# Attention of an adaLN block: batch loops written out on every engine, row sums inverted ahead of the tile copies

## The reference

```python
h = _layernorm(x, axis=-1) * (1 + ca) + sa
# attention on h
scores = jnp.einsum('bhqd,bhkd->bhqk', q, k) * scale + bias
attn = jax.nn.softmax(scores, axis=-1)
a = jnp.einsum('bhqk,bhkd->bhqd', attn, v)
...
x = x + ga * (a @ o_w.T)
h = _layernorm(x, axis=-1) * (1 + cb) + sb
x = x + gb * ffn(h)        # router, top 8 of 160 experts, shared expert
```

## Time and profile before

| | |
|---|---|
| median of 3 runs | 1016.47 us (1014.36 to 1022.89) |
| profiled execution | 1013.81 us, of which the span of the trace is 1012.0 |
| granted TensorE clock in it | 0.985 of 2.4 GHz |
| attention in the trace | from about 29 to 518 us; the experts from about 568 us to the end |
| DVE, ACT, POOL busy | 769.4, 679.4, 398.1 us |

### The profile page before, as it was taken

How to read it: one execution, slowest core, us unless ns; L and a number is a source line. 1 busy time by engine, 2 the same in 40 slices (tenths; PEclk the granted TensorE clock), 3 DMA queues, 4 the chain that set the end, 5 groups by cost and what they waited for, 6 DMA issues and landing times.

```text
span 1012.0 us, 16804 instructions
## 1 busy us (share of the span) xinstructions
PE 953.2 (94%) x4592; PEld 690.6 (68%) x4592; DVE 769.4 (76%) x1452; ACT 679.4 (67%) x1168; POOL 398.1 (39%) x260
## 2 busy tenths in 40 slices
PE   4889999899998999999969699999999999999997
PEld 2546666566665666666524578888888888888886
DVE  5757667566665666766647589999999999999997
ACT  3556666466665666666626477877777777777775
POOL 0578888688886888888910000000000000000000
PEclk9999999899999999999979899999999999999999
DMA  7885445256444445534200899999999999999991
GB/s 205 258 234 119 97 119 126 63 124 142 113 96 101 96 118 125 125 90 99 66 19 27 204 221 219 223 222 222 223 222 222 221 224 221 223 220 225 220 206 41
DMA packets 71096, 160.39 MB, mean 158 GB/s; under 512 B 10273, under 2 KB 36193, under 8 KB 60945
## 3 DMA queue, kind: packets, MB, share of 16 engines
q1 hardware_dynamic: 71056, 159.97, 70.1%
HBM read 105.60 MB, written 2.42 MB: 107 GB/s over the span
## 4 chain that ended last, share of the span: by engine, by line
PE 84%; DMA 4%; DVE 4%; issue 3%; ACT 2%; SPq 1%; POOL 1%; POOLq 0%; DVEq 0%; ACTq 0%
PE ps L620 40%; PE ps L433 11%; PE ps L420 10%; PE ps L409 5%; PE ps L411 5%; PE ps L383 4%; PE ps L446 3%; PE ps L394 2%; DMA strips<-in_L_ffn_w_down 2%; DMA k_low<-qk 1%; POOL prob L859 1%; DMA comb_rows<-strips 1%; PE ps L538 1%; PE ps L540 0%; DVE qk L959 0%
## 5 line engine op out<-in xcount | busy, mean ns | idle before, releaser
L859 POOL TENSOR_SCALAR prob<-prob,rinv 128x512 f32<-128x512 f32 x256 | 397.9, 1567 | 111.3 <-DVE rinv L993 109.1
L706 ACT ACTIVATE prob<-prob,nmax 128x512 f32<-128x512 f32 x256 | 182.9, 716 | 150.9 <-DVE nmax L976 150.8
L620 PE MATMUL ps<-hT,wT 128*128 128x512 f32 x960 | 244.2, 390 | 0.3 <-DVE wT L1145 0.3
L1164 DVE TENSOR_TENSOR PT<-v_sb,strips 128x1024 f32<-128x1024 f32 x160 | 196.0, 1225 | 41.4 <-ACT v_sb L830 28.3
L830 ACT ACTIVATE v_sb<-ps 128x1024 f32<-128x1024 f32 x160 | 164.5, 1028 | 77.9 <-PE ps L620 77.4
L620 PEld LDWEIGHTS ps<-hT,wT 128*128 128x128 f32 x960 | 180.8, 189 | 39.0 <-ACT strips L805 1.1
L620 PE MATMUL ps<-stack,wT 128*128 128x512 f32 x640 | 198.1, 391 | 9.2 <-DVE wT L1151 9.2
L204 DVE COPY PT<-ps 128x512 f32<-128x512 f32 x128 | 88.4, 691 | 141.2 <-PE ps L420 138.7
L1151 DVE TENSOR_TENSOR wT<-PT,stack 128x1024 fp32r<-128x1024 f32 x160 | 195.0, 1219 | 0.0
L976 DVE CUSTOM_DVE_ANT_0 prob<-ps,strips 128x512 f32<-128x512 f32 x256 | 165.0, 681 | 11.5 <-issue 8.0
L822 ACT CAST stack<-PT 128x1024 fp32r<-128x1024 f32 x160 | 166.6, 1041 | 8.8 <-DVE PT L1164 8.8
(11 more groups left out here) (105 smaller groups left out, 731.1 us busy)
## 6 DMA issues: line engine op xcount, KB each, us to landing
strips<-comb_rows SPq DMA_DIRECT2D x158, 512.0 KB, 10.9
stack<-qk SPq DMA_DIRECT2D x128, 256.0 KB, 3.8
k_low<-qk SPq DMA_DIRECT2D x64, 128.0 KB, 3.9
hT<-qk SPq DMA_DIRECT2D x64, 128.0 KB, 3.8
strips<-bias_rows SPq DMA_DIRECT2D x3, 1792.0 KB, 13.9
strips<-in_L_ffn_w_gate SPq DMA_DIRECT2D x80, 64.0 KB, 9.8
strips<-in_L_ffn_w_down SPq DMA_DIRECT2D x80, 64.0 KB, 11.0
strips<-bias_rows SPq DMA_DIRECT2D x2, 896.0 KB, 5.4
```

Source lines behind the costliest of these rows:

```text
L620: last = nc.tensor.matmul(ps[:, bank + c, :], weights(a), rows(m, c), start=start and k == 0, stop=stop and k == 2, skip_group_check=True)
L706: nc.scalar.activation(prob[:, u, :], prob[:, u, :], ACT.Exp, bias=nmax[:, u:u + 1], scale=-1.0, accum_out=rsum[:, u:u + 1]).then_inc(s_ex ...
L859: nc.gpsimd.tensor_scalar(prob[:, u, :], prob[:, u, :], rinv[:, u:u + 1], None, ALU.mult).then_inc(s_prob, 1)
L1164: nc.vector.tensor_tensor(weighted[:, k % 4, :], silu[:, k % 2, :], cb[:, r, half * HALF:(half + 1) * HALF], ALU.mult).then_inc(s_mul, 1)
```

## The change

Three things are edited. (1) The loops over b on the five engines become Python loops: the same instructions, written out three times (GpSimd: four times), with constants in place of registers. (2) On VectorE, in each slot the inversion of two row sums stands ahead of the copies of transposed tiles (and, in slot 0, of `copy_o`); before it stood behind them. (3) `update_x` and `new_statistics` of batch b move from the end of pair 9 into pair 2 of the next batch, behind its first two `add_bias`.

```diff
-            with dve.Fori(0, B - 1) as b:
+            for b in range(B - 1):
                 for n in range(2, HPAIRS + 2):
                     pair(b, n)
...
@@ VectorE, pair(b, n)
+                if n == 2 and b >= 1:
+                    update_x(b - 1)
+                    new_statistics(b - 1)
+                invert_sums(b, n, 0)
                 if n >= 2:
                     copy_o(b, n - 2)
                 if n >= 1:
                     copy_probs(b, n - 1, 5)
-                invert_sums(b, n, 0)
...
+                invert_sums(b, n, 2)
                 if n >= 1:
                     copy_probs(b, n - 1, 7)
-                invert_sums(b, n, 2)
...
+                invert_sums(b, n, 4)
                 copy_probs(b, n, 1)
-                invert_sums(b, n, 4)
...
+                invert_sums(b, n, 6)
                 copy_probs(b, n, 3)
-                invert_sums(b, n, 6)
                 if not (final and n >= HPAIRS - 2):
                     qk_low(b, n + 2)
-                if n == HPAIRS + 1:
-                    update_x(b)
-                    new_statistics(b)
```

More of the change, by code:

```diff
@@ L291, in _ @@
             sp.dma_start(ebias[0:E - P, 1:2], expert_bias[P:E, :]).then_inc(ld["small"], 16)
-            with sp.Fori(0, B - 1) as b:
+            for b in range(B - 1):
                 for n in range(2, HPAIRS + 2):
@@ L508, in _ @@
             pe.wait_ge(ld["ow"], 16)
-            with pe.Fori(0, B - 1) as b:
+            for b in range(B - 1):
                 for n in range(2, HPAIRS + 2):
@@ L760, in _ @@
             pair(0, 1)
-            with act.Fori(0, B - 1) as b:
+            for b in range(B - 1):
                 for n in range(2, HPAIRS + 2):
@@ L857, in normalise @@
                     pool.wait_ge(s_rinv, b * (G // 2) + (UNITS * n + u) // 2 + 1)
-                    pool.sem_inc(apart, 1)
                 nc.gpsimd.tensor_scalar(prob[:, u, :], prob[:, u, :], rinv[:, u:u + 1], None,
                                         ALU.mult).then_inc(s_prob, 1)
-            with pool.Fori(0, B) as b:
+            for b in range(B):
                 for n in range(HPAIRS):
```

## The result

The changed kernel takes 1018.48 us in the median of 20 runs, the kernel before 1014.56 in 20: a ratio of 1.0044, 95% interval 1.0023 to 1.0066. It is a little slower. In the profiled executions the span goes from 1012.0 to 1016.2 us. Afterwards nine variants were measured, two of them twice. The shortest are the change without its inversion in slot 0 (0.9844 and 0.9853 of the time before) and the change with no early inversion at all (0.9843 and 0.9873); their times are not told apart. For each variant the time is a median of 4 to 8 executions, the ratio is to the kernel before as measured beside it, and the span and all rows are those of one profiled execution. The ratios leave out the few executions that fell in the chip's slower state.

The account below looks back on a forecast made before the run. TensorE was taken to bound steady pairs of 14.20 us. Terms -15.5 + 2.4 + 16.8 + 0.5 = +4.2 us gave 1018.0 from the profiled execution, 1020.7 from the median; forecast 1019, range 1001 to 1030.

Parts of the forecast that it names:

- The ring: Slot 0's early reciprocal waits for the exponential, delaying `attend` each pair: 14.8 us instead of 14.20, +16.8 us over 28 pairs.
- Slot 1: VectorE's early reciprocal in slot 1, taken with slots 2 and 3: worth nothing in the steady pairs.
- The seams: Three pairs at batch boundaries: writing out the loops brings them down to steady pairs of 14.20 us, winning 15.5 us.
- The moved update: `update_x` and statistics in VectorE's pair 2: 1.07 us hidden in a wait, 0.8 us delay per batch boundary, +2.4 us.
- The pause inside straight code: VectorE's price for written-out loops: 0.24 us in six pairs, taken as hidden and costed at nothing.
- The end: Last two pairs of the attention, where GpSimd is the bound: +0.5 us, between 0.71 earlier and 1.2 later.
- The sum: Whole kernel: -15.5 + 2.4 + 16.8 + 0.5 = +4.2 us on the profiled execution of 1013.81 us.
- Slack unseen in the ring: Rival: VectorE and ScalarE have slack, steady pairs stay at 14.20 us; -13.8 us, 1000 to 1003; chance 0.20.
- A dearer stall through the clock: Rival: TensorE's clock or restarts make each 0.6 us stall cost 0.9; +12.6 us, 1026 to 1029; chance 0.17.
- Late code: Rival: three blocks of straight code reach VectorE late, 3.88 us each and some clock; +17, 1031 to 1034; chance 0.08.

## Why the prediction was right

**The ring** was forecast at 14.8 us and is 14.79. By its steps, `add_bias` 2 was to start 3.58 to 3.70 us after `add_bias` 0, and starts 3.56 after it (2.70 before). One step was off: the operation behind a waiting reciprocal starts 0.09 us after it (380.70 to 380.79), the 0.07 of the queued one and not the 0.19. Of the 0.07 us that the next pair was to gain from the early inversion of slot 3, only 0.02 came (from the copy of unit 3 to `add_bias` 0 it is 1.78 us, and was 1.80), for `qk_low` now starts where ScalarE's `qk_high` ends. That a delay comes back in each pair, once a slack of some 0.28 us is used up, is what three doses show: 0.25 us late costs nothing (between the copies), 0.86 late costs 0.59, and 0.86 late with both copies brought forward costs 0.10.

**Slot 1** was treated with slots 2 and 3 as free, though the wait for transposes was shown for those two alone. In the changed kernel the copy of unit 7 waits for the reciprocal and ends 0.16 us ahead of ScalarE's copy, so that moving it should have won nothing by itself (no run has that alone). The steps had it there ("ends at about the same time"), and the sum does not suffer; but it is a second path of the same delay, as the two kernels with an early copy of unit 6 show.

**The seams.** 15.5 us were to be won against steady pairs of 14.20. From 21.71, 20.86 and 15.76 to 15.24 or 15.25 each, 12.6 were. Each seam keeps 0.59 us of ring and 0.45 of update. The 0.45 is also in the rows: from `add_bias` 0 to the reciprocal it is 2.72 us at a seam (304.10 to 306.82) and 2.27 in a steady pair (378.43 to 380.70). The moved update is the term that was clearly mis-sized, 0.45 us a seam and not 0.8. It holds VectorE from 305.32 to 306.82, 1.50 us and not 1.84; written out, its statistics have no register instructions between them and come closer together.

**The pause inside straight code** was costed at nothing, by a row of 0.24 us, and as hidden. It is hidden where TensorE is the bound: the pair of the loops alone in which it comes (213.40) takes 14.20. In the changed kernel two of them cost 0.36 us each. The prediction said that it would be wrong if the pause came back in the straight code; what came is a tenth of the 3.88 us that it meant.

**The end** was to cost +0.5; from the last `project_qk` to the transposes of y it is 41.60 us (478.86 to 520.46) against 40.86 (476.72 to 517.58), so +0.7.

**The sum.** Forecast +4.2 us, and the span went from 1012.0 to 1016.2. The exact agreement is partly luck. From the first `project_qk` of the loop's pairs to the last of the attention it is 402.38 - 399.97 = 2.4 us, and 0.7 at the end: 3.1 that the sum was about. The update cost 1.1 less than forecast, and the ring 0.9 less, for this stretch has 27 pairs and not 28; the two pauses added 0.7, the end 0.2. The remaining 1 us of the span lies in the experts (+1.3) and ahead of the first of those `project_qk` (-0.3), which differ by some microseconds between executions. The forecast of 1019 rested besides on a base between the profiled execution and a median of three, 1016.47; the median of 20 is 1014.56, so that the change in the medians is 3.9.

**The rivals.** Slack unseen in the ring: there was some, about 0.28 us, and it was in the sum. A dearer stall through the clock: the clock is 1.00 in all windows of the changed kernel with 0.5 us idle in each pair. Late code: the only pauses without a named cause in VectorE's rows of the attention are the two of 0.27 us.

## What to carry to other kernels

Moving an operation ahead of others also moves its wait ahead of them. Before doing so, list what stood in front of it and ask of each place whether the engine waited there anyway: two of the four inversions here fell into such a wait and were free, a third was free as long as nothing ahead of it came later, and the fourth had no such wait and cost 16 us. An engine that is busy for only 68% of a pair can still hold the fastest one once per round; what counts is the slack of the ring through it, and that can be read off two timelines. And a change of several parts that moves the time by half a per cent can hold a part worth 1.5%: test the parts one by one.

## What the runs showed of the hardware

- VectorE's return to the start of its loop of 311 instructions (waits not counted) paused it for 3.77 to 3.88 us, and for 4.35 and 4.27 us with the inversions early. With TensorE's granted clock at 0.84 and 0.92 in the two stretches, this cost the seams of the kernel before 6.4 and 5.6 us (21.71 and 20.86 against 15.29 with the loops written out). Its loop over the experts, of 38 instructions, runs 18 times, and the profile before names no such pause in it. That length is the cause was not tried. The returns of ScalarE, TensorE, GpSimd and SP together showed 0.2 us.
- Away from returns VectorE has a pause of 0.24 to 0.37 us now and then. With the order alone, loops kept, it comes at the same place in each round of the loop, at 112.09, 237.84 and 363.50. In the changed kernel the two that show lie 283 us apart. No run tries its cause.
- Where TensorE waits for two engines, the named releaser can be the wrong one: with ScalarE's copy done 0.41 us and VectorE's 0.09 us ahead of `attend`, the row said ScalarE.
